# Softmax attention with every steady product cut into two 64-partition halves, and output banks copied out at once

## The chip, the cores and the metric

One Trainium2 chip, one core of it. The metric is the device time of one launch in microseconds; the kernel before takes 1138.88 us, the median of three runs (1138.76 to 1141.35). Smaller is better.

## The reference, cut to what matters

Four layers run one after the other on 1024 tokens of width 256: softmax attention, a mixture of experts, linear attention and a second mixture of experts, each after a layer norm. The change touches the first one only:

```python
xq = (x @ wq + bq)   # 1024 tokens, 16 heads of 128
xk = (x @ wk + bk)   # 4 key/value heads, each shared by 4 query heads
xv = (x @ wv + bv)
attn = softmax(einsum(xq / sqrt(128), xk))      # 16 heads, 1024 x 1024, over the keys
out = einsum(attn, xv).reshape(1024, 16 * 128)
return out @ wo + bo
```

## The kernel before

All times below are of `softmax_attention_phase` (line 223 on). float32 values are split into a rounded high part and a rest ("low"), both float32r, and every matrix product is three matmuls that accumulate in PSUM: high by high, high by low, low by high (`product`, lines 37 to 41). ScalarE makes the high part when it copies out of PSUM, VectorE subtracts it for the low part.

The order of the work is written out by hand as lists of events (lines 248 to 269), which every engine walks through in the same order (`laps`, line 351). There are four laps, one for each key/value head `g`. A lap has 8 units; a unit is one query head and 512 queries. The events are:

- `k`, `q`, `v`: a projection, 12 matmuls of 512 columns for `k` and `q`, 48 of 128 columns for `v` (lines 500 to 520). ScalarE copies it with its bias to `proj` and rounds it (lines 594, 603), VectorE takes the low part (line 654).
- `s`: half of the scores of a tile of 128 queries by 1024 keys, one product into one bank (line 527). After two of them VectorE takes the row maximum (line 686), ScalarE the exponential with its row sums (line 579), VectorE the inverse of the sums (line 647), and GpSimd multiplies the tile by it (line 422).
- `t`: a step of the transposes: for one block of 128 keys, four tiles of probabilities are transposed on TensorE (line 537) into one bank; ScalarE copies it to `pt_h` (line 612), VectorE puts the rest into `pt_l` (line 697). Even steps use bank 4 and odd ones bank 5; a step waits for the low part of the step before the last one (line 535).
- `p`: the product of such a step with the values, 512 queries wide, accumulated over the 8 steps of a unit in bank 6 or 7, alternating from unit to unit (lines 329, 548). After step 7 ScalarE copies the bank to `o_h` (line 622) and VectorE writes `o_l` from bank and copy (line 703).
- `y`: the output projection of half the tokens, 48 matmuls of 256 columns (line 557); VectorE adds it to `x` (line 215).

Banks 0 to 3 are two slots of two banks that `k`, `q`, `v`, `y` and score tiles take in turn; a job begins when the job two before it has been read (`begin`, line 472).

A steady block is: two `s` (a tile), two `p`, two `t`. The transposes run two blocks ahead of the products that use them. Before every eighth tile a `q` stands in front of the block. A lap has 26 such blocks, then a change to the next head in which `k`, `v` and `y` are put between the last `p` and `t` and the first `s` of the next head. The last lap ends with `closing`: the last seven pairs of `p` and five pairs of `t`, then `y`.

The code of the events, of the slots and of each engine's part follows.

Of the kernel before, what the change touches and what calls it, by code (L numbers as in the profile page):

```python
# [16 lines left out]
F32 = mybir.dt.float32  # L17
# [7 lines left out]
P = 128  # L25
# [197 lines left out]
def softmax_attention_phase(nc, net):  # L223
# [27 lines left out]
    opening = [("k",), ("q", 0), ("v",)] + [("s", s) for s in range(LEAD)] + [("vs",)] + pair("t", 0)  # L251
    steady = []
# [8 lines left out]
    change = [("k",)] + pair("p", at) + pair("t", at + 4) + [("v",)] + pair("p", at + 2) + pair("t", at + 6)  # L261
    for n in range(3):
        change += pair("s", 2 * n) + pair("p", at + 4 + 2 * n) + pair("t", at + 8 + 2 * n)
    change += pair("s", 6) + pair("p", at + 10) + pair("s", 8) + pair("p", at + 12)
    change += [("vs",)] + pair("s", 10) + [("y", 0)] + pair("t", 0) + [("y", 1)]
# [3 lines left out]
    closing += [("y", 0), ("y", 1)]  # L269

# [7 lines left out]
    with ExitStack() as mem:  # L278
# [17 lines left out]
        pt_h, pt_l = sb("pt_h", [P, PT, BANK], F32R), sb("pt_l", [P, PT, BANK], F32R)  # L296
        o_h, o_l = sb("o_h", [P, PER, T], F32R), sb("o_l", [P, PER, T], F32R)
        neg_max, row_sum, inv_sum = sb("neg_max", [P, TILES]), sb("row_sum", [P, TILES]), sb("inv_sum", [P, TILES])

        consts, ready = sem("consts"), sem("ready")  # L300
# [9 lines left out]
        o_high, o_split, y_full, y_added = sem("o_high"), sem("o_split"), sem("y_full"), sem("y_added")  # L310
# [14 lines left out]
        def turned(j):  # L325
            return ps[:, 4 + j % 2, :]

        def o_bank(u):
            return ps[:, 6 + u % 2, :]
# [21 lines left out]
        def laps(eng, run):  # L351
# [5 lines left out]
            run(KV - 1, [e for e in steady if e != ("q", PER)] + closing, first)  # L357

        def belongs_next(events, n):
            if events is opening:  # L360
                return True
            e = events[n]
            return ("k",) in events[:n] and e[0] in "vs" or e[0] == "k" or (e[0] == "t" and e[1] < 2)

        with nc.Block() as block:
# [31 lines left out]
            def _(pool):  # L397
# [49 lines left out]
                nc.gpsimd.memset(one[:, :], 1.0).then_inc(ready, 1)  # L447
                pool.sem_inc(wo_split, 1)
                pool.wait_ge(ready, 1)
# [4 lines left out]
                for c in range(DC):  # L454
                    pool.wait_ge(w_high, 2 + c)
                    nc.gpsimd.tensor_tensor(wq_l[:, c, :], wq_raw[:, c, :], wq_h[:, c, :].bitcast(F32), ALU.subtract)\
                        .then_inc(wq_split, 1)
                for t in range(LEAD // 2):
                    normalise(t + 1, t)
# [5 lines left out]
            def _(pe):  # L465
                def run(g, events, start):
                    jobs = jobs_of(events)
# [26 lines left out]
                    for place, e in enumerate(events):  # L494
# [5 lines left out]
                        if e[0] in "kq":  # L500
                            if e[0] == "k":
                                pe.wait_ge(wkv_split, g + 2)
                            elif start == 0 or e[1] == PER:
                                pe.wait_ge(wq_split, DC * (g + 2))
                            for b in range(NB):
                                cols = slice(b * BANK, (b + 1) * BANK)
                                for c in range(DC):
                                    hh = slice(e[1] % PER * DH, (e[1] % PER + 1) * DH) if e[0] == "q" else None
                                    wt = (wkv_h[:, 0, c, :], wkv_l[:, 0, c, :]) if e[0] == "k" else \
                                        (wq_h[:, c, hh], wq_l[:, c, hh])  # L510
                                    last = product(nc, slot(n, start)[:, b, :], *wt, xn_h[:, c, cols], xn_l[:, c, cols],
                                                   c == 0, c == DC - 1)
                            last.then_inc(proj_full, 1)
                        if e[0] == "v":
                            for i in range(TT):
                                toks = slice(i * P, (i + 1) * P)
                                for c in range(DC):
                                    last = product(nc, slot(n, start)[:, i // 4, (i % 4) * P:(i % 4 + 1) * P], xn_h[:, c, toks],
                                                   xn_l[:, c, toks], wkv_h[:, 1, c, :], wkv_l[:, 1, c, :], c == 0, c == DC - 1)
                            last.then_inc(values_full, 1)  # L520
                        if e[0] == "s":
                            t, b = divmod(e[1], 2)
                            hh, i = divmod(t, TT)
                            if e[1] % (2 * TT) == 0:
                                pe.wait_ge(proj_split, 2 + PROJ * own + hh)
                            keys = slice(b * BANK, (b + 1) * BANK)
                            last = product(nc, slot(n, start)[:, b, :], q_h[:, hh % 2, i * P:(i + 1) * P],
                                           q_l[:, hh % 2, i * P:(i + 1) * P], k_h[:, keys], k_l[:, keys], True, True)
                            if b == 1:
                                last.then_inc(s_full, 1)  # L530
                        if e[0] == "t":
# [1804 lines left out]
```

## Time and profile before

| | |
|---|---|
| median of three runs | 1138.88 us |
| the profiled execution | 1144.78 us, of which the span that the profile shows is 1142.9 us |
| TensorE busy | 1059.6 us, 93% of the span |
| VectorE, ScalarE, GpSimd busy | 751.3, 599.2, 564.3 us |
| matmuls | 6276 |

The profile shows one execution. PE is TensorE's matmul side and PEld its weight loads, which run beside the matmuls. DVE is VectorE, ACT is ScalarE, POOL is GpSimd. Matmuls are pipelined: one that is listed with 0.39 us begins 0.23 us after the one before it, so the distance from start to start is the cost, not the duration. A row of the timeline joins neighbours of one kind: its first figure is the start, the second the length of all of them together, and x8 their number. In "32*128 32x256" the first pair is the stationary operand (32 partitions, 128 columns), the second the moving one (32 partitions, 256 columns). The attention phase with its ending fills the span from about 20 us to 619 us.

### The profile page before, as it was taken

Reading aid. Unit: us, or ns where it says so; the run is one execution under the profiler, and the core shown is the slowest. Engines: PE = TensorE matmul, PEld = TensorE weight load, DVE = VectorE, ACT = ScalarE, POOL = GpSimd, SP = SyncE. Lnnn points to the kernel's source line nnn. Section 1 sums busy time; section 2 is a strip of 40 time slices with the busy share of each in tenths; the row PEclk is TensorE's granted clock in tenths of the full one; section 3 lists DMA queues with packets and bytes.
Section 4 is the critical chain, followed back from the end, with each engine's and each line's share of the span. In section 5 each row is a group of like instructions: output and inputs, shape, how many; then the busy total and the mean of one; then the engine's idle time right before and its main releaser. Section 6 shows DMA issues by size and latency. Waiting matters only on the chain. (4 is left out here: it accounts for less than half of the span.)

```text
span 1142.9 us, 16866 instructions
## 1 busy us (share of the span) xinstructions
PE 1059.6 (93%) x6276; PEld 893.9 (78%) x6276; DVE 751.3 (66%) x1312; ACT 599.2 (52%) x1027; POOL 564.3 (49%) x408
## 2 busy tenths in 40 slices
PE   5899999999999999999998899997977978999992
PEld 4788888888888888888886776654755778999992
DVE  4877665777457775667775644446778765777777
ACT  3566654666446665456662424333422255777772
POOL 1664623756136563355540347772314776644453
PEclk9999999999999999999999899999988998999997
DMA  8400210002501672000001146631200457666665
GB/s 198 49 29 1 54 40 1 19 10 46 48 1 40 209 216 52 1 1 1 1 1 39 43 146 217 212 125 55 106 2 5 157 190 239 205 226 222 224 208 203
DMA packets 45634, 109.84 MB, mean 96 GB/s; under 512 B 8519, under 2 KB 26069, under 8 KB 43504
## 3 DMA queue, kind: packets, MB, share of 16 engines
q1 hardware_dynamic: 38640, 95.46, 29.1%
q0 software_dynamic: 6912, 13.30, 3.1%
q8 instruction: 50, 0.82, 0.3%
q14 instruction: 32, 0.26, 0.1%
HBM read 94.27 MB, written 41.29 MB: 119 GB/s over the span
## 5 line engine op out<-in xcount | busy, mean ns | idle before, releaser
L422 POOL TENSOR_TENSOR at_prob<-at_prob,at_inv_sum 128x1024 f32<-128x1024 f32 x128 | 243.6, 1905 | 286.4 <-DVE at_inv_sum L647 286.4
L612 ACT ACTIVATE at_pt_h<-ps 128x512 fp32r<-128x512 f32 x256 | 139.1, 596 | 152.4 <-PE ps L537 152.3
L697 DVE TENSOR_TENSOR at_pt_l<-ps,at_pt_h 128x512 fp32r<-128x512 f32 x256 | 164.6, 685 | 64.5 <-ACT at_pt_h L612 64.5
L686 DVE TENSOR_REDUCE at_neg_max<-ps 128x1 f32<-128x1024 f32 x128 | 154.7, 1209 | 36.3 <-PE ps L41 35.9
L579 ACT ACTIVATE at_prob<-ps,at_neg_max 128x1024 f32<-128x1024 f32 x128 | 143.6, 1122 | 17.9 <-DVE at_neg_max L686 17.9
L537 PE MATMUL ps<-ident,at_prob 128*128 128x128 f32 x1024 | 133.8, 274 | 3.8 <-POOL at_prob L422 3.8
L2072 POOL DMA_INDIRECT lines<-f_y,f_x_raw x96 | 97.1, 1011 | 81.0 <-ACT f_y L1990 51.9
L537 PEld LDWEIGHTS ps<-ident,at_prob 128*128 128x128 f32 x1024 | 120.1, 141 | 21.1 <-POOL at_prob L422 4.7
L39 PE MATMUL ps<-at_k_h,at_q_h 128*128 128x512 f32 x256 | 109.0, 426 | 0.0
L39 PE MATMUL ps<-at_pt_h,at_v_h 128*128 128x512 f32 x256 | 101.1, 395 | 0.0
L41 PE MATMUL ps<-at_pt_h,at_v_l 128*128 128x512 f32 x256 | 100.8, 394 | 0.0
L41 PE MATMUL ps<-at_k_h,at_q_l 128*128 128x512 f32 x256 | 100.8, 394 | 0.0
L40 PE MATMUL ps<-at_k_l,at_q_h 128*128 128x512 f32 x256 | 100.6, 393 | 0.0
L40 PE MATMUL ps<-at_pt_l,at_v_h 128*128 128x512 f32 x256 | 100.2, 392 | 0.0
L1023 POOL TENSOR_TENSOR f_act<-f_act,f_cw_row 128x1024 f32<-128x1024 f32 x32 | 77.5, 2424 | 35.8 <-DVE f_act L1058 29.2
L1058 DVE SCALAR_TENSOR_TENSOR f_act<-ps,f_relu 128x1024 f32<-128x1024 f32 x34 | 41.6, 1223 | 57.2 <-ACT f_relu L964 57.2
L964 ACT ACTIVATE f_relu<-ps 128x1024 f32<-128x1024 f32 x36 | 36.8, 1022 | 72.4 <-PE ps L41 72.4
L39 PE MATMUL ps<-f_x_h,f_e_h 128*128 128x384 f32 (+1 forms) x192 | 67.1, 349 | 3.9 <-DVE f_x_l L2188 2.0
L41 PE MATMUL ps<-f_x_h,f_e_l 128*128 128x384 f32 (+1 forms) x192 | 64.8, 338 | 0.0
L40 PE MATMUL ps<-f_x_l,f_e_h 128*128 128x384 f32 (+1 forms) x192 | 64.8, 337 | 0.0
L2059 POOL DMA_INDIRECT slots<-f_row,f_slot_of x48 | 51.1, 1065 | 20.1 <-issue 13.1
L926 PE MATMUL ps<-f_act,f_e_raw 128*128 128x512 f32 x128 | 59.7, 593 | 0.0
(308 smaller groups left out, 2546.7 us busy)
## 6 DMA issues: line engine op xcount, KB each, us to landing
e_raw<-in_we SPq DMA_DIRECT2D x32, 624.0 KB, 4.2
f_cw_row<-cw SPq DMA_DIRECT2D x32, 512.0 KB, 3.9
slots<-in_empty SPq DMA_DIRECT2D x4, 3456.0 KB, 43.9
f_x_raw<-slots SPq DMA_DIRECT2D x32, 432.0 KB, 4.8
lines<-in_empty SPq DMA_DIRECT2D x3, 2048.0 KB, 32.8
f_e_raw<-in_we SPq DMA_DIRECT2D x32, 128.0 KB, 2.2
at_wq_raw<-in_wq SPq DMA_DIRECT2D x4, 512.0 KB, 3.7
at_wo_raw<-in_wo SPq DMA_DIRECT2D x4, 512.0 KB, 3.5
```

The source lines that it names most:

```text
L39: nc.tensor.matmul(out, lhs_h, rhs_h, start=start, stop=False)
L40: nc.tensor.matmul(out, lhs_h, rhs_l, start=False, stop=False)
L41: return nc.tensor.matmul(out, lhs_l, rhs_h, start=False, stop=stop)
L422: nc.gpsimd.tensor_tensor(prob[:, t % RING, :], prob[:, t % RING, :], inv_sum[:, t:t + 1].broadcast_to([P, T]), ALU.mult).then_inc(normed, 1)
L537: last = nc.tensor.transpose(turned(e[1])[:, i * P:(i + 1) * P], prob[:, (4 * u + i) % RING, kt * P:(kt + 1) * P], net.ident[:, :])
L579: nc.scalar.activation(halves(prob[:, t % RING, :]), slot(k, start), ACT.Exp, bias=neg_max[:, t:t + 1], accum_out=row_sum[:, t:t + 1]).the ...
L612: nc.scalar.activation(pt_h[:, e[1] % PT, :], turned(e[1]), ACT.Copy).then_inc(pt_high, 1)
L686: nc.vector.tensor_reduce(neg_max[:, t:t + 1], slot(n, start), AX.XY, ALU.max, negate=True).then_inc(maxed, 1)
L697: nc.vector.tensor_tensor(pt_l[:, e[1] % PT, :], turned(e[1]), pt_h[:, e[1] % PT, :].bitcast(F32), ALU.subtract).then_inc(pt_split, 1)
L926: last = nc.tensor.matmul(ps[:, 4 + b, :], e_raw[:, m, 1, :], act_of(m)[:, cols], start=first, stop=final)
L1023: nc.gpsimd.tensor_tensor(act_of(r), act_of(r), cw_row[:, r % ROWS, :], ALU.mult).then_inc(weighed, 1)
L2072: nc.gpsimd.indirect_dma_start(out=net.lines, out_offset=bass.IndirectOffsetOnAxis(ap=line_of, axis=0), in_=y[:, n % YRING, b, :], in_offs ...
```

## The change

Every product in the steady part and in the change between laps is cut along the contraction: instead of one matmul over 128 partitions, one over partitions 0 to 63 and one over partitions 64 to 127. Two results are worked on at the same time, in two banks: while the first bank gets its upper halves, the second gets its lower halves, and halfway (in a later event) they change. The second event of such a pair is the old second one for `s` and `p`, and a new event `r` ("rest") for `k`, `q`, `v` and `y`. A new semaphore `halved` makes TensorE wait, before a second half, until its first half has ended.

- `s`: the two events of a tile each do 12 half matmuls of 512 columns, six for each bank; the first event starts both banks, the second ends them.
- `p`: the moving operand is cut into two groups of 256 queries, one for each of banks 6 and 7 (`outputs`). An event does 12 half matmuls of 256 columns, so a pair 24 instead of 6 of 512. Both banks now serve every unit; the first `p` of a unit waits until the outputs of the unit before have been copied out.
- `t`: a step is 8 transposes of 64 partitions, with the 64 by 64 part of the identity as the moving operand, instead of 4 of 128: lower partitions into bank 4, upper ones into bank 5. A pair of steps fills both banks, and the semaphore `pt_full` rises by 2 at its end. The pair waits for the low parts of all steps before it.
- Outputs: ScalarE copies both output banks to a new buffer `o_full` at once, then rounds `o_full` to `o_h`; VectorE takes the low part later, from `o_full`, after the next pair of `t` (for the last unit of a lap at once).
- Order: `s p s p t t` instead of `s s p p t t`. A `q` is begun before the `t` pair of the block ahead of its old place, and its rest follows that pair. In the closing the order is `p t p t`.
- The opening keeps whole projections and the closing whole `y`; a wait of GpSimd on its memset is replaced by one on `wkv_split`.

```diff
@@ helpers
+HROWS = P // 2
+def upper(r):
+    return slice(r * HROWS, (r + 1) * HROWS)
+def half_products(nc, turn, outs, lhs_h, lhs_l, rhs_h, rhs_l, start, stop):
+    passes = [(lhs_h, rhs_h), (lhs_h, rhs_l), (lhs_l, rhs_h)]
+    for n, (lhs, rhs) in enumerate(passes):
+        for r in range(2):
+            j = r ^ turn
+            last = nc.tensor.matmul(outs[j], lhs[j][upper(r)], rhs[j][upper(r)], start=start and turn == 0 and n == 0,
+                                    stop=stop and turn == 1 and n == len(passes) - 1)
+    return last
@@ events
+    def woven(a, b):
+        return [a[0], b[0], a[1], b[1]]
+    def query(s):
+        return ("q", (s // 2 + 2) // TT) if (s // 2 + 2) % TT == 0 and s < STEPS else None
+    steady = woven([query(LEAD), rest(*query(LEAD))], pair("s", LEAD))
     for s in range(LEAD, STEPS, 2):
-        if (s // 2 + 2) % TT == 0:
-            steady.append(("q", (s // 2 + 2) // TT))
-        steady += pair("s", s)
         if s > LEAD:
-            steady += pair("p", s - LEAD - 2)
-        steady += pair("t", s - LEAD + 2)
+            steady += woven(pair("s", s), pair("p", s - LEAD - 2))
+        ahead = query(s + 2)
+        steady += ([ahead] if ahead else []) + pair("t", s - LEAD + 2) + ([rest(*ahead)] if ahead else [])
...
+    change = woven([("k",), rest("k")], pair("p", at)) + pair("t", at + 4)
+    change += woven([("v",), rest("v")], pair("p", at + 2)) + pair("t", at + 6)
...
+    change += [("vs",)] + pair("s", 10) + [("y", 0)] + pair("t", 0) + [rest("y", 0), ("y", 1), rest("y", 1)]
     closing = []
     for n in range(at, STEPS, 2):
-        closing += pair("p", n) + (pair("t", n + 4) if n + 4 < STEPS else [])
+        closing += woven(pair("p", n), pair("t", n + 4)) if n + 4 < STEPS else pair("p", n)
@@ TensorE, s
+                            if b:
+                                pe.wait_ge(halved, halves_of[g, ("s", 2 * t)])
+                            at_ = slot(slot_of["s", 2 * t], start)
+                            last = half_products(nc, b, [at_[:, j, :] for j in range(NB)],
+                                                 [q_h[:, hh % 2, i * P:(i + 1) * P]] * NB, [q_l[:, hh % 2, i * P:(i + 1) * P]] * NB,
+                                                 [k_h[:, j] for j in keys], [k_l[:, j] for j in keys], True, True)
@@ TensorE, t
-                            pe.wait_ge(pt_split, LIFT + own * STEPS + e[1] - 1)
+                            if kt % 2 == 0:
+                                pe.wait_ge(pt_split, LIFT + own * STEPS + e[1])
                             for i in range(4):
-                                last = nc.tensor.transpose(turned(e[1])[:, i * P:(i + 1) * P],
-                                                           prob[:, (4 * u + i) % RING, kt * P:(kt + 1) * P], net.ident[:, :])
-                            last.then_inc(pt_full, 1)
+                                at = kt % 2 * D + i * HROWS
+                                for h in range(2):
+                                    last = nc.tensor.transpose(turned(h)[:, at:at + HROWS],
+                                                               prob[upper(h), (4 * u + i) % RING, kt * P:(kt + 1) * P],
+                                                               net.ident[upper(h), upper(h)])
+                            if kt % 2:
+                                last.then_inc(pt_full, 2)
@@ TensorE, p
-                            if kt == 0:
-                                pe.wait_ge(o_split, LIFT + g * UNITS + u - 1)
-                            pe.wait_ge(pt_split, LIFT + g * STEPS + e[1] + 1)
-                            keys = slice(kt * P, (kt + 1) * P)
-                            product(nc, o_bank(u), v_h[:, keys], v_l[:, keys], pt_h[:, e[1] % PT, :], pt_l[:, e[1] % PT, :],
-                                    kt == 0, kt == KT - 1).then_inc(pv_done, 1)
+                            if turn:
+                                pe.wait_ge(halved, halves_of[g, ("p", e[1] - 1)])
+                            elif kt:
+                                pe.wait_ge(pv_done, LIFT + g * STEPS + e[1])
+                            elif g * UNITS + u:
+                                pe.wait_ge(o_moved, 2 * (g * UNITS + u) - 1)
+                            if not turn:
+                                pe.wait_ge(pt_split, LIFT + g * STEPS + e[1] + 2)
+                            for step in (e[1] - turn, e[1] - turn + 1):
+                                kt = step % KT
+                                keys = slice(kt * P, (kt + 1) * P)
+                                last = half_products(nc, turn, [outputs(0), outputs(1)], [v_h[:, keys]] * 2, [v_l[:, keys]] * 2,
+                                                     moving(pt_h, step), moving(pt_l, step), kt == 0, kt == KT - 1)
@@ ScalarE, outputs
                             act.wait_ge(pv_done, LIFT + g * STEPS + e[1] + 1)
-                            nc.scalar.activation(o_h[:, u // NB, (u % NB) * BANK:(u % NB + 1) * BANK], o_bank(u),
-                                                 ACT.Copy).then_inc(o_high, 1)
+                            act.wait_ge(o_split, LIFT + g * UNITS + u)
+                            nc.scalar.activation(queries(o_full[:, :]), all_outputs(), ACT.Copy).then_inc(o_moved, 1)
+                            act.wait_ge(o_moved, 2 * (g * UNITS + u) + 1)
+                            nc.scalar.activation(o_h[:, u // NB, (u % NB) * BANK:(u % NB + 1) * BANK], o_full[:, :],
+                                                 ACT.Copy).then_inc(o_moved, 1)
```

## Rows read from the trace of the kernel before

**Rows 1.** The page: busy time and share of TensorE.

```profile
PE 1059.6 (93%) x6276; PEld 893.9 (78%) x6276; DVE 751.3 (66%) x1312; ACT 599.2 (52%) x1027; POOL 564.3 (49%) x408
```

**Rows 2.** Busy us by stretch: PE, PEld, DVE, ACT, POOL (instructions), PEclk, DMA share, GB/s.

```profile
335.80:483.40 147.60, 147.18 (x847) 126.77 (x846) 98.56 (x147) 84.64 (x147) 72.63 (x46) 1.00 0.36 100
```

**Rows 3.** Timeline of PE, one steady block: start, length, operation.

```profile
388.44 1.04 PE L537 MATMUL ps<-ident,at_prob 128*128 128x128 f32 x8
389.23 0.48 PE L39 MATMUL ps<-at_k_h,at_q_h 128*128 128x512 f32 x1
...
390.71 0.39 PE L39 MATMUL ps<-at_pt_h,at_v_h 128*128 128x512 f32 x1
...
392.08 0.60 PE L537 MATMUL ps<-ident,at_prob 128*128 128x128 f32 x4
```

**Rows 4.** Instructions of one line: duration ns min/median/max, first and last start.

```profile
L889 PEld LDWEIGHTS ps<-ident,f_cw x8: 97/97/98, 652.5 to 653.4; 128*32 128x32 f32 x8
L537 PEld LDWEIGHTS ps<-ident,at_prob x1024: 137/140/231, 40.8 to 602.3; 128*128 128x128 f32 x171
L1867 PEld LDWEIGHTS ps<-f_router,f_xn x32: 186/193/338, 874.2 to 878.8; 128*128 128x128 f32 x32
```

**Rows 5.** Timeline of PE: eight transposes with 32 weight columns.

```profile
652.71 1.04 PE L889 MATMUL ps<-ident,f_cw 128*32 128x128 f32 x8
```

**Rows 6.** Timeline of PE: two rounds of four 32-partition matmuls in four banks.

```profile
815.10 0.39 PE L1336 MATMUL ps<-la_q_p,la_k_t 32*128 32x256 f32 x4
815.31 0.39 PE L1336 MATMUL ps<-la_q_p,la_k_t 32*128 32x256 f32 x4
```

**Rows 7.** Timeline of PE: float32 (not float32r) matmuls over the whole array.

```profile
722.25 1.88 PE L926 MATMUL ps<-f_act,f_e_raw 128*128 128x512 f32 x4
```

**Rows 8.** Timeline of PE: float32r matmuls of 256 columns in the last y.

```profile
608.16 0.28 PE L40 MATMUL ps<-at_wo_l,at_o_h 128*128 128x256 f32 x1
...
608.52 0.28 PE L40 MATMUL ps<-at_wo_l,at_o_h 128*128 128x256 f32 x1
```

**Rows 9.** Timeline of PE: matmuls of 32 columns, each with a load of 128 columns.

```profile
874.24 1.83 PE L1867 MATMUL ps<-f_router,f_xn 128*128 128x32 f32 x15
```

**Rows 10.** Timeline of PE, ACT and DVE around a q.

```profile
402.96 1.03 PE L537 MATMUL ps<-ident,at_prob 128*128 128x128 f32 x8
403.59 1.09 ACT L612 ACTIVATE at_pt_h<-ps 128x512 fp32r<-128x512 f32 x2 [1.45 <-PE ps L537]
403.75 0.48 PE L39 MATMUL ps<-xn_h,at_wq_h 128*128 128x512 f32 x1
...
404.22 1.29 DVE L697 TENSOR_TENSOR at_pt_l<-ps,at_pt_h 128x512 fp32r<-128x512 f32 x2 [0.77 <-ACT at_pt_h L612]
404.56 1.12 ACT L579 ACTIVATE at_prob<-ps,at_neg_max 128x1024 f32<-128x1024 f32 x1
405.56 0.21 ACT L579 ACTIVATION_READ_ACCUMULATOR at_prob<-ps,at_neg_max 128x1 f32 x1
...
406.63 0.39 PE L39 MATMUL ps<-at_k_h,at_q_h 128*128 128x512 f32 x1
```

**Rows 11.** Timeline of ACT: an output copy from PSUM, a copy from SBUF.

```profile
392.27 0.60 ACT L622 ACTIVATE at_o_h<-ps 128x512 fp32r<-128x512 f32 x1 [1.02 <-PE ps L41]
...
407.98 1.06 ACT L603 ACTIVATE at_q_h<-at_proj 128x1024 fp32r<-128x1024 f32 x1
```

**Rows 12.** Timeline of PE and DVE in the closing.

```profile
589.59 1.04 PE L537 MATMUL ps<-ident,at_prob 128*128 128x128 f32 x8
...
601.61 1.04 PE L537 MATMUL ps<-ident,at_prob 128*128 128x128 f32 x8
...
606.06 0.69 DVE L703 TENSOR_TENSOR at_o_l<-ps,at_o_h 128x512 fp32r<-128x512 f32 x1 [1.90 <-ACT at_o_h L622]
606.90 0.36 PE L39 MATMUL ps<-at_wo_h,at_o_h 128*128 128x256 f32 x1 [1.50 <-DVE at_o_l L703]
```

**Rows 13.** Busy us by stretch, as rows 2, around TensorE's one long gap in steady work.

```profile
304.00:310.00 6.00, 4.47 (x20) 3.65 (x20) 1.22 (x1) 0.00 (x0) 0.00 (x0) 0.72 0.23 26
```

More of the change, by code:

```diff
@@ L249, in pair, with rest @@
         return [(kind, s), (kind, s + 1)]
-    opening = [("k",), ("q", 0), ("v",)] + [("s", s) for s in range(LEAD)] + [("vs",)] + pair("t", 0)
-    steady = []
+    def rest(*e):
+        return ("r", e)
+    def woven(a, b):
+        return [a[0], b[0], a[1], b[1]]
+    def query(s):
+        return ("q", (s // 2 + 2) // TT) if (s // 2 + 2) % TT == 0 and s < STEPS else None
+    opening = [("k",), ("q", 0), ("v",), ("s", 0)]
+    for s in range(2, LEAD, 2):
+        opening += [("s", s), ("s", s - 1)]
@@ L323, in slot, with turned, stored, moving @@
             return ps[:, 2 * k:2 * k + 2, :]
[L325 to L329, printed above, removed]
+        def turned(h):
+            return ps[:, 4 + h, :]
+        def stored(pt, step):
+            return pt[:, step // 2 % (PT // 2), step % 2, :]
+        def moving(pt, step):
+            return [pt[:, step // 2 % (PT // 2), h, step % 2 * D:(step % 2 + 1) * D] for h in range(2)]
+        def queries(ap):
+            return ap.rearrange("p (i h q) -> p h i q", i=4, h=2)
+        def outputs(h):
+            return ps[:, 6 + h, 0:D]
+        def all_outputs():
+            return ps[:, 6:8, 0:D].rearrange("p h (i q) -> p h i q", i=4)
         def halves(ap):
@@ L356, in laps @@
                 run(g, steady + change, first)
-            run(KV - 1, [e for e in steady if e != ("q", PER)] + closing, first)
+            run(KV - 1, [e for e in steady if e not in (("q", PER), rest("q", PER))] + closing, first)
         def belongs_next(events, n):
@@ L499, in run @@
                             n += 1
-                        if e[0] in "kq":
+                            slot_of[e] = n
+                        job = e[1] if e[0] == "r" else e
+                        turn = int(e[0] == "r")
+                        done = whole(events, e)
+                        if turn:
+                            pe.wait_ge(halved, halves_of[g, job])
+                            place_ = slot(slot_of[job], start)
+                        elif e in jobs:
+                            place_ = slot(n, start)
@@ L501, in run @@
+                        if job[0] in "kq":
                             if e[0] == "k":
                                 pe.wait_ge(wkv_split, g + 2)
-                            elif start == 0 or e[1] == PER:
+                            elif e[0] == "q" and (start == 0 or e[1] == PER):
                                 pe.wait_ge(wq_split, DC * (g + 2))
-                            for b in range(NB):
-                                cols = slice(b * BANK, (b + 1) * BANK)
-                                for c in range(DC):
[L508 to L520, printed above, removed]
+                            cols = [slice(b * BANK, (b + 1) * BANK) for b in range(NB)]
@@ L561, in _ @@
+                            if done:
+                                last.then_inc(y_full, 1)
+                            else:
+                                half_done(last, g, e)
                 for s in lifted["pe"]:
@@ L586, in run @@
                             n += 1
-                        if e[0] in "kq":
+                            slot_of[e] = n
+                        done = whole(events, e)
+                        if done and done[0] in "kq":
                             exps()
-                            count = proj_count(g, e)
+                            count = proj_count(g, done)
                             act.wait_ge(proj_full, count)
@@ L605, in run @@
                             exps()
-                            waiting.append((own, e[1] // 2, n))
+                            waiting.append((own, e[1] // 2, slot_of["s", e[1] - 1]))
                         if e[0] == "t":
@@ L659, in run @@
                             n += 1
-                        if e[0] in "kq":
-                            later.append(e)
+                            slot_of[e] = n
+                        done = whole(events, e)
+                        if done and done[0] in "kq":
+                            later.append(done)
                             if start == 0:
                                 lows()
-                        if e[0] == "v":
+                        if done and done[0] == "v":
                             dve.wait_ge(values_full, own + 1)
```

144 lines of the change are left out of this document (105 added, 39 removed).

## The prediction

> **What bounds the kernel now.** I began with the page's first part: TensorE is busy for 93% of the span [rows 1]. The busy table by stretch then gives the third lap of the attention: TensorE is busy for 147.18 of 147.60 us at a granted clock of 1.00 (2.4 GHz), VectorE for 98.56, ScalarE for 84.64, GpSimd for 72.63 [rows 2]. The timeline shows the block that repeats: 3.64 us from one pair of transposes to the next, with no wait on TensorE [rows 3]. So what TensorE does in a block sets the time until another engine's chain becomes longer; the other engines have a third of their time free.
>
> The block splits into three. The eight transposes are 0.11 us apart ((1.04 - 0.27) / 7), and the first matmul behind them still waits for its weights (0.48 us instead of 0.39), so `t` costs 0.87. `p` costs 392.08 - 390.71 = 1.37 for six matmuls (0.228 each), and `s` the rest, 1.40 (0.233 each) [rows 3].
>
> **Transposes.** What limits a transpose at 0.11 us? Not its load: with 32 weight columns they are as far apart ((1.04 - 0.27) / 7 = 0.11) as with 128 [rows 3, 5]. It is the 128 moving columns. The change makes 16 of 64 partitions with 64 moving columns, two at a time in two banks, so eight rounds of half the columns: 0.055 a round. The load has to keep up. A transpose's load takes 97 ns for 32 columns and 140 for 128 [rows 4], so 0.45 ns a column, 57 ns for 128, in two row groups at once. That loads and matmuls of different row groups do run at once is shown by the four-row matmuls: four start together, and the next four 0.21 us later, which is what one such matmul costs over the whole array (256 columns; 512 cost (1.88 - 0.59) / 3 = 0.43, half of it 0.215) [rows 6, 7]. I take 0.060 a round: 0.48, and 0.05 for the longer load that follows, 0.53 instead of 0.87. Bounds: 0.055, and 0.11 if the load takes what other loads take (193 ns long, their matmuls 0.11 apart although they move only 32 columns) [rows 4, 9].
>
> That last bound is also a page's rule: the Trainium skill, "TensorE: Matmul & The Clock Gate", section "LDWEIGHTS (loading the stationary operand)", prices a load by its columns at 1.2 GHz whatever its rows, which is 107 ns here, and makes the transposes no faster. This trace's ordinary loads agree with it, its transposing loads (140 against 193 ns) speak against it.
>
> **Products.** Twice the matmuls, two at a time, is the same number of columns streamed. In `s` six rounds of 512 columns: the tiled rounds above showed neither gain nor loss against the whole array, so 0.233 a round stays, 1.40. Bounds: 0.215 (the tiled round of rows 6, whose type is float32, where the stream is half as dense) and 0.24. In `p` each round has only 256 columns, and such matmuls are (608.52 - 608.16) / 3 = 0.12 apart [rows 8]: 12 x 0.12 = 1.44 instead of 1.37. The lower bound is the load's 0.111 ((1.83 - 0.28) / 14) [rows 9]. `q`, `k`, `v` and `y` keep their rates and rounds.
>
> A block is then 1.40 + 1.44 + 0.53 = 3.37, 0.27 less. There are 32 pairs of `t` in each of three laps and 26 in the last one's steady part: 122 x 0.27 = **33 us gained** (41 in `t`, 8 lost in `p`).
>
> **What the new order costs.** First the chain from `t` to the next `t`, since a pair now waits for both low parts and `pt_full` comes only at its end. From the start S of `t`: last transpose at S + 0.43, ended S + 0.70, ScalarE's copies from S + 0.73, VectorE's lows 0.63 later for 1.29 [rows 10], done at S + 2.65, against the next `t` at S + 3.37. Covered by 0.7. The row maximum, now a quarter block later, still ends before the next lows.
>
> *Outputs.* ScalarE copies twice (0.60 from PSUM; half of 1.06 from SBUF [rows 11]) with a wait between, ahead of the `t` copies, which begin at about S + 1.40 instead of S + 0.73. The lows end at S + 3.32 and the next `t` wants S + 3.37: about 0.05 a unit, 1.5 in all. The first `p` of a unit waits for the first copy alone (S + 0.85), and comes at S + 1.2. VectorE's late low part falls into its free time.
>
> *Queries.* Here I expect the dearest loss. The `s` after a `q` waits for the exponential of the tile two jobs before, and with `q` in between that is the tile of the block just done. ScalarE does it after both `t` copies. Before: `t` starts at 402.96, the exponential starts at 404.56 and its sums are read by 405.77, while `q` keeps TensorE until 406.63 [rows 10]. After, only half of `q` (6 x 0.235 = 1.41) stands behind `t`: from S, TensorE is done at S + 0.53 + 1.41 = 1.94, and the exponential at S + 0.73 + 0.97 + 1.21 + 0.04 = 2.95. That is 1.0 us idle, at the second to fourth `q` of three laps and two of the last: **11 x 1.0 = 11 us**.
>
> *Ends.* Twice in a change a rest follows its first half with nothing between (`s` 10 and 11, `y` 1): TensorE waits for the end of the last matmul and loads anew, 0.35 each; and `y` 0 waits for an exponential that stands behind the second output copy, 0.4 more. 1.1 x 3 = 3.3. In the closing there is no `s` to cover the copies. From the last transpose of a pair the next may start 0.27 + 0.03 + 0.63 + 1.29 + 0.05 = 2.27 later, and half a pair, one `p` half and half a pair follow, less a round: 0.24 + 0.72 + 0.24 - 0.06 = 1.14. So 3.4 a pair, five times 17.0, where the rows give 601.61 - 589.59 = 12.0 [rows 12]. With the second output copy ahead of the last low part (0.69, on which `y` already waited 1.50) and two bare halves it is 6 us in all.
>
> Losses: 1.5 + 11 + 3.3 + 6 = 22. **The sum is -11 us.** Against the profiled execution, 1144.8, that is 1134; that execution lies 5.9 above the median of the runs, and the same difference taken from 1138.9 gives **1128**. GpSimd, at about half its time, gets shorter blocks, but a normalised tile has more than one microsecond to spare; I cost it at nothing. Without that cover each late tile costs what it is late, once a unit.
>
> **Rivals.**
> - *The gap between products goes too.* A float32r matmul of 512 columns costs 0.228 to 0.235, a float32 one 0.215 for the same stream [rows 3, 7]. If two row groups fill each other's gaps, `s` is 6 x 0.215 = 1.29 and `p` 12 x 0.111 = 1.33, a block 3.15, 0.49 less: 60, and 5 in `q` and `y`. Then the output chain shows (0.3 a unit, 9 instead of 1.5) and a `q` waits 1.15, so losses are 31: -34, 1105. For it: the tiled rounds have no gap. Against: neither have whole-array ones of that type. 28%.
> - *The transposes don't halve.* The load of 128 columns decides: rounds of 0.11, `t` 0.93, a block 0.13 longer. 122 x 0.13 = 16 lost, and the 22, and 2 more in the closing: +40, **1179**. The sign turns where a round costs over 0.071 (11 us over 976 rounds). For it: a load over 193 ns in every other form. Against: the transposing loads of 140. 12%.
> - *The clock falls in the new gaps.* After TensorE's one gap of some 1.5 us in steady work the granted clock averaged 0.72 over six microseconds, so part of it at 1.2 GHz [rows 13]; that cost about 1.7. If each of the 16 new gaps did so, it is 27 more: +16, 1155. Against: these gaps are shorter. 7%.
> - *The gain is eaten.* Rounds of 0.065 and stalls half as large again give about nothing, 1139. 10%.
>
> **How the numbers follow.** The forecast has 43%, its own range 1118 to 1134 (`t` rounds 0.055 to 0.066, stalls by a third). With the first rival 71% are faster, one of them on the edge of no change, so 70% faster, 10% within 0.3% (3.4 us, about what a measurement of this kernel can tell from no change), 20% slower. The range takes in the first rival and reaches up to between no change and the clock's case: 1103 to 1150.
>
> **What would show it.** The profile after should have pairs of `t` whose 16 transposes take about 0.75 us from first start to last end, `s` rounds at 0.23 and `p` rounds at 0.12, blocks of 3.37, eleven gaps of 1 us before an `s` that wait for the exponential, and five closing pairs 3.4 apart. `t` rounds at 0.11 would make the forecast wrong at its root; `s` rounds at 0.215 would make it too timid; gaps at `s` or `t` in ordinary blocks would mean that the chain through ScalarE and VectorE has become the bound.

## The result, and the profile after

The changed kernel takes 1172.57 us (median of 4 runs, 1166.43 to 1177.66) against 1140.12 beside it on the same chip (4 runs): the ratio is 1.028, interval 1.022 to 1.034. It is slower by 32 us where 11 us less was forecast. The profiled execution has a span of 1173.5 us.

The profile page and the waits up to the end of the attention, for TensorE:

```profile
PE 1043.0 (89%) x11020; PEld 905.2 (77%) x11020; DVE 751.7 (64%) x1312; ACT 619.6 (53%) x1059; POOL 564.0 (48%) x408
```

```profile
PE ps L61 <- issue: 26.2, 7, 10.4
PE ps L61 <- ACT at_prob L711: 10.4, 13, 0.8
PE ps L643 <- DVE at_pt_l L846: 8.9, 12, 1.5
PE ps L643 <- POOL at_prob L483: 4.1, 1, 4.1
PE ps L643 <- issue: 1.1, 1, 1.1
```

In each row stand what waited and what it waited for, then the us in total, the number of times and the longest. Against [rows 1] TensorE is busy 17 us less and the span is 31 us longer. The gain in work is there, and waits took more than it. The largest is new: 27.3 us in eight gaps that end on "issue", that is, on nothing which the profile shows.

First the steady block, TensorE's timeline; it answers to [rows 3]:

```profile
251.80 0.66 PE L643 MATMUL ps<-ident,at_prob 64*128 64x64 f32 x16
252.26 0.48 PE L61 MATMUL ps<-at_k_h,at_q_h 64*128 64x512 f32 x2
252.58 0.39 PE L61 MATMUL ps<-at_k_l,at_q_h 64*128 64x512 f32 x2
...
253.05 0.28 PE L61 MATMUL ps<-at_pt_h,at_v_h 64*128 64x256 f32 x2
253.16 0.28 PE L61 MATMUL ps<-at_pt_l,at_v_h 64*128 64x256 f32 x2
...
255.15 0.53 PE L643 MATMUL ps<-ident,at_prob 64*128 64x64 f32 x12
```

From pair to pair 3.35 (255.15 - 251.80), forecast 3.37. `t` takes 0.55: 0.46 to the first product, whose next round comes 0.32 later instead of 0.23. Two halves of a `p` pass take 0.117, so `p` 1.40; a round of `s` takes 0.23. Between the two pairs stand 52 matmuls with the 16 of one `t`, where the kernel before has 20. (An event of `s` has 6 half matmuls, three for each bank, and not the 12 and six of the list of the change.)

Then the largest gap, on the same timeline, and the stretch around it (columns as [rows 2]):

```profile
305.23 0.27 PE L61 MATMUL ps<-at_pt_l,at_v_h 64*128 64x256 f32 x1
315.93 0.37 PE L61 MATMUL ps<-at_pt_l,at_v_h 64*128 64x256 f32 x1 [10.42 <-issue]
315.93 0.58 PE L61 MATMUL ps<-at_pt_h,at_v_l 64*128 64x256 f32 x2
316.31 0.63 PE L61 MATMUL ps<-at_k_h,at_q_h 64*128 64x512 f32 x2
316.74 0.63 PE L61 MATMUL ps<-at_k_l,at_q_h 64*128 64x512 f32 x2
```

```profile
300.00:320.00 20.00, 9.00 (x108) 8.04 (x110) 5.98 (x9) 6.13 (x11) 3.79 (x2) 0.74 0.57 66
```

The gap lies between the two halves of one round, where the program has no wait, so no semaphore of the order can be its cause. When TensorE resumes its clock has fallen to 1.2 GHz: rounds of `s` are 0.43 apart instead of 0.23, up to 319.3. The gaps of 6.93 and 4.42 at 138 and 156 have the same behind them, 3 to 5 us at half clock each.

What moved then? The DMA view, two stretches of the changed kernel (queue, kind: packets, MB, share of 16 engines), first before the gap, then from 288 to 312:

```profile
q1 hardware_dynamic: 288, 0.26, 1.8%
q8 instruction: 6, 0.10, 0.9%
```

```profile
q1 hardware_dynamic: 1732, 2.13, 67.4%
q14 instruction: 1, 0.01, 0.2%
```

Queue 8 carries instructions in packets of 16 KB, and they are TensorE's: 87 packets for 11020 matmuls and as many weight loads here, 50 for 6276 of each before, which is 253 and 251 instructions a packet. In the 47.5 us before the hole, six packets came; their starts are 7 to 11 us apart. From 288 to 312 there is none: the last came at 286.60, the next at 312.91, three microseconds before TensorE went on. SP had issued a bulk fill at 287.27 (`lines` cleared in DRAM, 2 MB, 32 us to landing). The kernel before has the same fills and such a hole too, 258.70 to 304.25, and goes on 2.2 us behind it:

```profile
306.47 0.41 PE L41 MATMUL ps<-at_wkv_h,xn_l 128*128 128x128 f32 x1 [1.53 <-issue]
```

That is its one gap of 1.53 us [rows 13]. In its steady part it needs a packet only every 22 us or so.

Two counts tie the gaps to the packets. Each of the eight gaps ends 2.2 to 3.0 us after the start of a packet. And they open after 441, 2968, 3221, 7271, 10057, 10311, 10816 and 11069 instructions (matmuls and loads that had begun): the distances are multiples of 253, one packet's worth, within 3. TensorE stops where a packet ends. After the last packet before the hole it still began 491 instructions, in the kernel before 535, about two packets' worth each. With 104 instructions in 3.38 us two packets last 16 us, with 40 in 3.63 us 46 (estimates from these counts); so the kernel before nearly bridges a hole that stops the changed one.

### The profile page after: what moved, and what is told of

Same layout as the page of the kernel before. It is cut to its first block and busy times, and to the rows that moved or that the text cites. A ratio compares the mean times of both kernels' runs of the same rounds, so it can differ in the third digit from the quotient of the medians.

```text
span 1173.5 us, 26511 instructions
## 1 busy us (share of the span) xinstructions
PE 1043.0 (89%) x11020; PEld 905.2 (77%) x11020; DVE 751.7 (64%) x1312; ACT 619.6 (53%) x1059; POOL 564.0 (48%) x408
## 5 line engine op out<-in xcount | busy, mean ns | idle before, releaser
L61 PE MATMUL ps<-at_pt_l,at_v_h 64*128 64x256 f32 x1024 | 150.1, 279 | 12.2 <-issue 12.2
L61 PE MATMUL ps<-at_pt_h,at_v_h 64*128 64x256 f32 x1024 | 152.3, 283 | 2.6 <-ACT at_o_full L757 1.2
L61 PE MATMUL ps<-at_pt_h,at_v_l 64*128 64x256 f32 x1024 | 150.7, 280 | 0.0
L61 PE MATMUL ps<-at_k_h,at_q_h 64*128 64x512 f32 x512 | 114.0, 434 | 9.7 <-ACT at_prob L711 8.2
L61 PEld LDWEIGHTS ps<-at_pt_l,at_v_h 64*128 64x128 f32 x1024 | 103.4, 187 | 12.6 <-issue 3.1
L61 PEld LDWEIGHTS ps<-at_pt_h,at_v_h 64*128 64x128 f32 x1024 | 103.2, 187 | 11.3 <-ACT at_o_full L757 1.3
L61 PEld LDWEIGHTS ps<-at_pt_h,at_v_l 64*128 64x128 f32 x1024 | 103.6, 187 | 10.6 <-issue 10.6
L61 PE MATMUL ps<-at_k_h,at_q_l 64*128 64x512 f32 x512 | 103.9, 394 | 0.4 <-issue 0.4
L61 PE MATMUL ps<-at_k_l,at_q_h 64*128 64x512 f32 x512 | 103.2, 391 | 0.0
L643 PE MATMUL ps<-ident,at_prob 64*128 64x64 f32 x2048 | 88.8, 225 | 14.1 <-DVE at_pt_l L846 8.9
L61 PEld LDWEIGHTS ps<-at_k_h,at_q_h 64*128 64x128 f32 x512 | 51.5, 189 | 18.2 <-ACT at_prob L711 12.9
```

The lines of the kernel that those rows point to most:

```text
L61: last = nc.tensor.matmul(outs[j], lhs[j][upper(r)], rhs[j][upper(r)], start=start and turn == 0 and n == 0, stop=stop and turn == 1 and n ...
L643: last = nc.tensor.transpose(turned(h)[:, at:at + HROWS], prob[upper(h), (4 * u + i) % RING, kt * P:(kt + 1) * P], net.ident[upper(h), upp ...
```

## The experiments

All times were taken beside the kernel before, in three groups, the first two on one chip and the third on another: its median was 1142.24 in the first (experiments 1, the first pacing and the transposes of 5), 1145.12 in the second (the second pacing, 3, the old closing of 6) and 1142.53 in the third (4, the paced transposes of 5, `q` behind `t`). A ratio is one of mean times within a group; kernels of different groups are compared by their ratios or their traces. "Last add" is the start of the last addition of `y` to `x` in the profiled execution, the end of the attention's products; before has 618.57, the change 649.88. Issue gaps are those of TensorE's matmul side within the attention.

| kernel | median us | ratio (interval) | last add | issue gaps |
|---|---|---|---|---|
| late fills, changed | 1249.93 | 1.095 (1.092 to 1.098) | 618.02 | 0 |
| late fills, before | 1247.79 | 1.093 (1.091 to 1.095) | 615.15 | 0 |
| first pacing, changed | 1147.02 | 1.005 (1.003 to 1.008) | 624.61 | 0 |
| transposes alone halved | 1147.19 | 1.004 (1.002 to 1.005) | 622.47 | 3.8 |
| second pacing, changed | 1144.22 | 0.9995 (0.998 to 1.001) | 618.32 | 0 |
| second pacing, before | 1140.52 | 0.996 (0.994 to 0.998) | 616.57 | 0 |
| products cut by columns | 1167.75 | 1.019 (1.015 to 1.024) | 641.03 | 7.0 |
| pieces in bursts, changed | 1163.43 | 1.018 (1.014 to 1.023) | 636.60 | 12.9 |
| halved transposes, paced | 1140.02 | 0.997 (0.996 to 0.999) | 614.35 | 0 |
| paced, q behind t | 1133.72 | 0.992 (0.990 to 0.995) | 608.84 | 0 |
| paced, q behind t, old closing | 1126.01 | 0.985 (0.980 to 0.989) | 600.63 | 0 |

**1. Fills moved behind the attention**, in the changed kernel and in the one before.

```diff
-                    sp.dma_start(net.lines...[g], ...).then_inc(net.slots_empty, 16)
-                empty_slots(sp, net)
@@ linear_attention_phase, SyncE, at its end
+                for g in range(3):
+                    sp.dma_start(net.lines...[g], ...).then_inc(net.slots_empty, 16)
+                empty_slots(sp, net)
```

> The changed kernel, but the seven bulk fills of DRAM (3 of lines, 4 of slots, 20 MB in all) are issued in the linear attention phase instead of during the softmax attention. Theory (TensorE starved of instructions while the fills write): the gaps before matmuls that the profile puts down to 'issue' (26.2 us in 7 gaps, the longest 10.4) vanish, and with them the stretches at half clock behind them (about 10 us); the last y ends near 614 us instead of 650, two blocks lie 3.37 apart throughout, the q gaps of 0.8 to 1.2 us stay. Rival (the doubled stream is too dense in itself, whatever the DMA does): the issue gaps stay near 26 us and the last y near 650. The total is not the test: moved fills may be late where they are needed, by up to 20 us.

> The kernel before with the fills moved in the same way, as the control. Both theories: one issue gap (1.5 us) and about 2 us of half clock go, so the last y ends 3 to 4 us earlier, near 615 instead of 618.6. Whatever the total changes beyond that is the price of the late fills, and is to be taken from the other run.

Both totals are some 106 us worse, because what comes after the attention then waits for the fills; only the attention is compared. TensorE's longest waits from 20 to 620 us, changed kernel:

```profile
PE ps L61 <- ACT at_prob L708: 11.2, 14, 0.8
PE ps L640 <- DVE at_pt_l L843: 10.1, 13, 1.5
```

No issue gap is left, the attention's end moves from 649.88 to 618.02 and before's from 618.57 to 615.15 (expected 614 and 615). So nearly all of the loss hangs on the fills, and without them the change is still 2.9 us behind instead of 11 ahead.

**2. Fills in 56 pieces** (24 of 256 KB, 32 of 432 KB), each waiting for one more normalised tile. In the first pacing SP stood at pieces while the next `wq` was wanted; the second issues all weights ahead of the pieces:

```diff
+                def fill(count):
+                    sp.wait_ge(normed, count)
+                    ...
                 for g in range(KV - 1):
...
                     load(g + 1, "q")
-                    sp.dma_start(net.lines...[g], ...).then_inc(net.slots_empty, 16)
+                    for count in (range(3, 10) if g == 0 else range(g * TILES - 6, g * TILES + 9)):
+                        fill(count)
...
```

> The changed kernel with the same fills at about the same time, but in 56 pieces (24 of lines with 256 KB, 32 of slots with 432 KB), each issued when GpSimd has normalised one more tile. Theory (an instruction fetch waits behind a long fill): no piece is long enough to starve TensorE, issue gaps under 5 us in sum, total 1135 to 1145. Rival (any DMA load at the same time slows the fetch): gaps of the same sum as with bulk fills, total 1165 to 1175.

> The changed kernel with the seven bulk fills cut into 56 pieces, one per normalised tile, and every weight load issued ahead of the pieces. Theory A (TensorE starves for instructions only while a bulk fill writes): no gap of TensorE that ends on nothing (issue) is over 0.6 us, the 4.5 us wait for the late weights of the first paced version is gone too, the last y is added to x at about 618.0 us (as in the kernel with the fills moved away), total 1138 to 1142. Theory B (the first pacing worked because its pieces lay at lucky places): issue gaps of 1 us and more are back somewhere, total 1150 or more.

> The kernel before with the same pieces instead of its bulk fills. Theory A: it only loses its one gap of 1.53 us and the half clock behind it; last y added at 615.2 instead of 618.6, total 1135 to 1137, so that the change is worth -3 to +5 us when neither kernel starves. Theory B (the pieces cost something of their own, such as slower loads): total 1139 or more.

The first pacing took the issue gaps away and made one of its own: TensorE waited 4.5 us for GpSimd, which had waited for `wq` behind the pieces. The second has neither; its last add comes at 618.32 as expected, its median is 2 us above the expected range. The first lies 2 us above its own. The second kernel's stretch and its DMA queues where the changed kernel had its worst gap, 300 to 320 and 288 to 312:

```profile
300.00:320.00 20.00, 20.00 (x314) 18.66 (x314) 13.13 (x20) 10.00 (x18) 5.69 (x3) 1.00 0.15 48
```

```profile
q1 hardware_dynamic: 192, 1.33, 18.2%
q8 instruction: 3, 0.05, 1.0%
```

Instructions come again, TensorE is busy all the time at a granted clock of 1.00. The medians of this pair, 1144.22 and 1140.52, put the change without starvation at +3.7 us, their traces at +1.8. Before with pieces came out at 1140.5 where 1135 to 1137 was expected: the runs of before stood 5 us higher in this group than beside the change, and the ratio says 0.4% gained. The last add (616.57) is 1.4 later than the expected 615.2.

**3. Products cut by columns** in the kernel before: twice the matmuls of `s` and `p`, no halves, no new order.

```diff
+def product_by_columns(nc, out, lhs_h, lhs_l, rhs_h, rhs_l, start, stop):
+    for c in range(2):
+        part = slice(c * D, (c + 1) * D)
+        last = product(nc, out[:, part], lhs_h, lhs_l, rhs_h[:, part], rhs_l[:, part], start and c == 0, stop and c == 1)
+    return last
```

> The kernel before, with every product of scores and of values cut in two by columns (256 instead of 512 moving columns, all 128 partitions, one at a time) and the bulk fills where they were: 32 matmuls a block instead of 20, with no halves by partitions and no change of order. Theory A (the number of instructions per time is what starves TensorE behind a bulk write): issue gaps of several us appear at 125 to 160, 274 to 310 and behind 367 us, 10 to 30 us in all, and the granted clock falls to half behind them; steady blocks 3.65 to 3.8 us. Rival B (the partition halves themselves, two matmuls 3 ns apart, outrun the fetching or its queue): no more issue gaps than the kernel before has, one of about 1.5 us; total is then the block's own change alone.

Its waits on the matmul side:

```profile
PE ps L40 <- issue: 4.8, 1, 4.8
PE ps L39 <- issue: 2.2, 1, 2.2
```

Blocks are 3.74, so 122 x 0.11 = 13 us is the block's own; 7.0 us are issue gaps, fewer than the 10 to 30 expected, but at the old places (160 and 304 us) and without any half. With whole fills the gaps go with the packets that queue 8 carries in the whole run: 50 gave 1.5 us of gaps, 58 (halved transposes) 3.8, 62 (columns) 7.0, 87 (the change) 27.3, one profile each.

**4. The same pieces, not paced.**

```diff
+                    for _ in range(8):
+                        fill()
```

Here `fill` has no wait for a normalised tile.

> The changed kernel with the bulk fills cut into the same 56 pieces, but issued in bursts at the old places (eight and eight and eight pieces of lines, then 32 of slots), so that they run back to back and none waits for a tile. Theory A (what starves TensorE is that the DMA engines stand full of bulk writes for 30 us and more while it runs through its instructions twice as fast; the pacing helps because an instruction fetch never waits behind more than one piece): issue gaps as in the changed kernel, 10 us and more in all, total 1155 or more. Rival (the size or shape of a single transfer decides, a piece is harmless however many follow): no issue gap over 0.6 us, total 1142 to 1146 as with the paced pieces.

```profile
PE ps L61 <- issue: 12.9, 6, 5.8
```

Pieces back to back starve TensorE again, as theory A had it, if half as long as whole fills: its instruction packets have holes of 18.1 and 22.0 us (133.33 to 151.43, 279.76 to 301.78) where the change has 22.4 and 26.3. All six gaps open after instruction counts at which gaps of the change open (3221, 7271, 10057 and so on), though 7 to 13 us earlier. By the last add, cutting alone is worth 13.3 us (649.88 - 636.60) and spacing the pieces another 18.3 (to 618.32). This kernel was run only twice.

**5. Transposes alone halved**, in the kernel before, products whole and in the old order, with bulk fills and with pieces.

```diff
-                            for i in range(4):
-                                last = nc.tensor.transpose(turned(e[1])[:, i * P:(i + 1) * P], ...)
+                            for i in range(4):
+                                for h in range(2):
+                                    last = nc.tensor.transpose(turned(h)[:, ...], prob[upper(h), ...], net.ident[upper(h), upper(h)])
```

> The kernel before with only the transposes cut into halves (16 of 64 partitions, pairs of steps in banks 4 and 5), all products whole, order and outputs as before. A block gains 0.34 in the transposes and pays two changes of the tiling per pair; at the one such change that the trace of before shows (from the four-row matmuls to whole products) the next start came 0.09 late. If that is the whole price, a block is 3.63 - 0.34 + 0.2 = 3.5 and the total 1122 to 1128. If a change costs 0.2 or more, nothing is left: 1138 and above, and the cutting of the products was needed for the gain. Issue gaps should stay under 4 us, since the stream grows by 8 matmuls a block instead of 32.

> The kernel before with its transposes alone cut into halves (products whole, order as before) and the paced pieces. Without starvation it shows what the cheapest part of the change is worth. Theory A: blocks of 3.59 against 3.63 us, 122 x 0.04 = 5 us gained, less 6 x 0.45 in the closing and 0.35 us a lap at the first pair: total 1137 to 1139, no faster than the kernel before with paced pieces by more than 3 us, since entering and leaving the halved form costs 0.3 us a block of the 0.36 gained. Rival: the entry cost was an effect of the starved instruction stream; the blocks fall to 3.37, total below 1120.

The block is 3.59 in both, and starvation has nothing to do with it: of the two outcomes foreseen it is the one in which nothing is left. TensorE's timeline at the two borders of a `t` pair:

```profile
394.81 0.23 PE L572 MATMUL ps<-ident,at_prob 64*128 64x64 f32 x2
394.97 0.50 PE L44 MATMUL ps<-at_k_h,at_q_h 128*128 128x512 f32 x1
395.30 0.39 PE L45 MATMUL ps<-at_k_l,at_q_h 128*128 128x512 f32 x1
...
397.59 0.39 PE L46 MATMUL ps<-at_pt_h,at_v_l 128*128 128x512 f32 x1
397.91 0.71 PE L572 MATMUL ps<-ident,at_prob 64*128 64x64 f32 x16
398.55 0.50 PE L44 MATMUL ps<-xn_h,at_wq_h 128*128 128x512 f32 x1
```

The last whole matmul before `t` takes 0.32 (397.91 - 397.59) where 0.23 is the rule, and the sixteen transposes up to the next product 0.64 instead of the 0.46 of the changed kernel. Those 0.09 and 0.18 are 0.27 of the 0.33 (0.79 - 0.46) which halving them gives, unless the neighbours are halved too. That is what the change bought with its many small instructions. In time this kernel stands beside before with pieces (ratios 0.997 and 0.996), its median 1 us above what was expected.

**6. The order.** Each `q` and its rest whole behind the pair of `t`; then also the closing as before, `p p t t`.

```diff
-        steady += ([ahead] if ahead else []) + pair("t", s - LEAD + 2) + ([rest(*ahead)] if ahead else [])
+        steady += pair("t", s - LEAD + 2) + ([ahead, rest(*ahead)] if ahead else [])
@@ closing, in the last kernel only
-        closing += woven(pair("p", n), pair("t", n + 4)) if n + 4 < STEPS else pair("p", n)
+        closing += pair("p", n) + (pair("t", n + 4) if n + 4 < STEPS else [])
```

> The changed kernel with paced pieces and each q with its rest behind its pair of t, closing as in the change. It parts the two edits of the fastest kernel so far (18.2 us under the paced changed kernel). Theory A, by the laps of that trace (142.5 against 145.3 us, so 0.93 a q): 11 x 0.93 = 10 us of it come from the q, total 1133 to 1135, the closing gives the other 6 to 8. Rival: the q gives nearly all and the closing under 3, total 1128 to 1130.

> As the kernel before in this list, and besides each q with its rest stands whole behind its pair of t, and in the closing both p come ahead of both t. Theory A (the order costs what the trace shows): the wait of 0.82 us for an exponential after a q is gone at all 11 places, 11 x 0.7 = 7.7 us; the pairs of the closing are 2.7 instead of 2.97 to 3.57 apart, about 3.5 us in all; last y added to x at about 607, total 1127 to 1131, which is faster than both kernels. Rival: the exponential is late for a whole q too (its chain, not its cover, decides) and the closing is bound by the chain from lows to transposes, so no more than 3 us come back, total 1136 to 1140.

Both edits together gave 18.2 us (1144.22 - 1126.01, one group). The `q` with its rest gave 9.5 of it by the last adds and 8 by the ratios, which stem from different groups; by the laps (145.32 to 142.53 us) it is 0.93 each. The closing gave 8.2 by the last adds and 9 by the ratios. The traces show 6.8 of it from the last steady `t` on, and 1.5 of these in the last `y` (11.66 instead of 13.15 us from its first matmul to the last add): the granted clock stays at 1.00 there, where it fell to 1.2 GHz for 3.4 us in the kernel with the change's closing. The total lies 1 us under the expected range, the last add 6 us before the expected 607. TensorE's waits from 20 us to the last `y`, for the last kernel:

```profile
PE ps L658 <- DVE at_pt_l L861: 4.4, 10, 0.9
PE ps L658 <- POOL at_prob L498: 4.1, 1, 4.1
PE ps L61 <- ACT at_prob L726: 2.2, 3, 0.7
PE ps L39 <- DVE at_o_l L802: 2.2, 1, 2.2
```

The exponential is waited for only at the three `y` 0, 2.2 us instead of 11.3 (in the paced kernel with the change's order). This kernel beats the one before by 1.5% (0.980 to 0.989), and is 14.5 us under before with pieces (taken in the same group, 1140.52). It was run four times.

## Why the prediction was wrong

The prediction is taken here step by step.

**The step that failed** is one that is not in the sum. "Twice the matmuls, two at a time, is the same number of columns streamed" prices the columns right, and takes for nothing what the added instructions cost (52 matmuls a block instead of 20). The text counts matmuls and rounds and never what brings them to TensorE; SP's bulk fills stand in none of its parts, though [rows 13] showed the one gap on "issue" in a kernel that ran with half the instructions. I took that gap only as a test of the clock. It was the first sign of the mechanism. Moving the fills away takes 31.9 us from the changed kernel and 3.4 from the one before: 28 of the 31 between their last adds, the gaps themselves and the half clock behind the long ones. It alone turns the sign. A second step failed by less, the stalls of the new order, priced at 22 us: without any starvation 13.9 us are missing, most of them there, and they eat the forecast gain. The slower side was given 20%, for the load and the clock; neither brought it.

**Transposes**: right. Rounds of 0.06, and 0.55 for `t` where 0.53 was forecast. What the Trainium skill says in "TensorE: Matmul & The Clock Gate", section "LDWEIGHTS (loading the stationary operand)", a load priced by its columns alone and so no faster transposes, doesn't hold for these: two loads of 128 columns every 0.06 us. **Products**: right, 0.117 (forecast 0.12) and 0.233; no gap between products closes in `s`, so the rival of 28% is refuted. The block came to 3.35 to 3.38. What the text didn't know is that transposes halved alone would have given only 0.04 (experiment 5).

**Queries**: right in mechanism and nearly in size. ScalarE's exponential and TensorE's `s` behind a `q` in the changed kernel:

```profile
236.91 1.12 ACT L711 ACTIVATE at_prob<-ps,at_neg_max 128x1024 f32<-128x1024 f32 x1
...
238.17 0.50 PE L61 MATMUL ps<-at_k_h,at_q_h 64*128 64x512 f32 x2 [0.82 <-ACT at_prob L711]
```

Idle for 0.82 to 0.83 where 1.0 was forecast, at ten of the eleven places here and at all of them in the paced kernel, and 0.93 came back when it was undone.

**Outputs**: undersized. With 0.05 a unit the text looked at the chain of a unit alone. In two blocks of a lap the copies and the low part of a `q` stand in the same queues. DVE's timeline in the paced changed kernel:

```profile
81.72 2.01 DVE L816 TENSOR_TENSOR at_q_l<-at_proj,at_q_h 128x1024 fp32r<-128x1024 f32 x1
83.65 1.28 DVE L861 TENSOR_TENSOR at_pt_l<-ps,at_pt_h 128x512 fp32r<-128x512 f32 x2
```

The next `t` waited 0.37 for those lows. Such blocks take 4.24 and 3.90 instead of 3.37, 1.4 a lap; another, of 4.37, is in the last lap. With 0.3 more in the change between heads and 0.2 in the `q`, a lap gains 2.2 where the terms give 4.1 (32 x 0.27 - 0.4 - 3.0 - 1.1).

**Ends**: the closing's pairs are 3.5 apart as forecast (3.4), one 4.5 because the next unit's `p` waited 1.18 for the output copy: 18.0 against 12.0, forecast 17.0. Behind the last pair 4.0 were lost where 1.0 was forecast. Part is the wait for the last low part, 2.17 instead of 1.50, and part the clock. TensorE in the last `y`, changed kernel with late fills:

```profile
605.41 0.28 PE L41 MATMUL ps<-at_wo_h,at_o_l 128*128 128x256 f32 x1
605.53 0.28 PE L39 MATMUL ps<-at_wo_h,at_o_h 128*128 128x256 f32 x1
605.65 0.34 PE L40 MATMUL ps<-at_wo_l,at_o_h 128*128 128x256 f32 x1
605.78 0.42 PE L41 MATMUL ps<-at_wo_h,at_o_l 128*128 128x256 f32 x1
605.99 0.42 PE L39 MATMUL ps<-at_wo_h,at_o_h 128*128 128x256 f32 x1
```

The granted clock over 604.8 to 610.8 is 0.72; rounds go from 0.12 to 0.21 for 3.4 us, about 1.6 us lost. It fell after the closing's run of gaps of 0.9 to 2.2 us, and after none of the eleven of 0.82. The length of a gap alone doesn't tell: it fell after the one of 1.53 in the kernel before, and not after one of 1.78 in the changed kernel (ended at 416.1). That rival (7%) was thus right in one place of its sixteen.

The sum for the two kernels with late fills: three laps 5.7 short of the forecast, the opening 1.6 (not in the sum; its cause I didn't look for), the last part 6.6 (2.1 in its steady blocks, 1.0 and 3.0 in the closing and behind it, the rest not assigned): 13.9, which takes -11 to the measured +2.9.

**What stays open**: that an instruction packet is late, and that TensorE stops where the packet before it ends, is read in the traces; that it takes dense instructions and bulk writes together is shown by experiments 1 to 4. Why a packet waits 20 us and more while packets of the fills go on was not tried, nor whether it matters that all fills read the same few rows of DRAM.

## What to carry to other kernels

An edit that multiplies small instructions on a busy engine must be weighed against the supply of instructions: count the packets of its instruction queue, look for "issue" gaps while bulk transfers run, and space such transfers by progress of the work, with every load that someone waits for issued first. A form of matmul that pays only when its neighbours have it too must be costed with its borders. Where a change weaves jobs together, look at each block that has two guests in the copying engines' queues, not at the steady one.

## What the runs showed of the hardware

- Under a 2 MB DRAM fill (DMA share 67%) no 16 KB instruction packet of TensorE came for 26.3 us; TensorE stood for 10.42 us and then ran 3.4 us at half clock. In pieces of 256 and 432 KB that are spaced by tiles, none of it was seen.
- A packet holds some 253 matmuls and weight loads. All eight gaps opened at such a boundary and ended 2.2 to 3.0 us after the start of a packet; 491 (changed kernel) and 535 (before) instructions still began after the last packet before the longest hole.
- Two halves of a product in two row groups (partitions 0 to 63 and 64 to 127) start together and together cost what one whole product does: 0.23 a round of 512 columns, 0.12 of 256. Two half transposes of 64 columns do the work of a whole one in 0.06 instead of 0.11. Between whole and halved matmuls lies a border: 0.09 us at the last whole one, 0.18 in the transposes behind it.
